# Order of a visit's output sums against the next weight part, in the last expert stage of a two-layer attention and expert kernel

## The reference, cut to what matters

```python
logits = jnp.einsum('btd,de->bte', x, Wg) + bg
top2_vals, top2_idx = jax.lax.top_k(logits, 2)
scores = jax.nn.softmax(top2_vals, axis=-1)
combine = jnp.einsum('btk,btke->bte', scores, one_hot(top2_idx))
h = gelu(jnp.einsum('btd,edh->bteh', x, W1) + b1)
y = jnp.einsum('bteh,ehd->bted', h, W2) + b2
out = jnp.einsum('bted,bte->btd', y, combine)
return _layer_norm(x + out, gamma, beta)
```

## Time and profile before

| | |
|---|---|
| median of 3 runs | 1300.97 us (1296.85 to 1301.41) |
| the profiled execution | 1300.37 us |
| its span, first to last instruction | 1298.6 us |
| mean granted TensorE clock over the span | 0.91 of full speed |
| PE matmul busy | 1131.4 us, 87% of the span |
| VectorE busy | 902.9 us, 70% |
| ScalarE busy | 790.0 us, 61% |
| GpSimd busy | 650.6 us, 50% |

### The profile page before, as it was taken

How to read it: one execution, slowest core, us unless ns; L and a number is a source line. 1 busy time by engine, 2 the same in 40 slices (tenths; PEclk the granted TensorE clock), 3 DMA queues, 4 the chain that set the end, 5 groups by cost and what they waited for, 6 DMA issues and landing times.

```text
span 1298.6 us, 23742 instructions
## 1 busy us (share of the span) xinstructions
PE 1131.4 (87%) x8184; PEld 1039.9 (80%) x8184; DVE 902.9 (70%) x1943; ACT 790.0 (61%) x1597; POOL 650.6 (50%) x581
## 2 busy tenths in 40 slices
PE   3789999998869999999988971999999999999950
PEld 2688787887858888888877861999999999999940
DVE  5677887676666666666637755787878787787847
ACT  3756566644235565565627640887878777787836
POOL 2435443443253666555443776255665745445326
PEclk8658999879999999999997865999999999999985
DMA  6544332221333778666647742568888776666649
GB/s 223 182 148 151 136 139 98 74 98 50 119 119 115 195 220 233 177 166 173 155 87 240 224 138 74 175 137 197 187 184 204 172 193 174 165 156 185 176 87 241
DMA packets 147497, 206.69 MB, mean 159 GB/s; under 512 B 29137, under 2 KB 121425, under 8 KB 140337
## 3 DMA queue, kind: packets, MB, share of 16 engines
q1 hardware_dynamic: 111376, 161.87, 38.1%
q0 software_dynamic: 35040, 42.75, 19.2%
q10 hardware_dynamic: 960, 0.54, 0.1%
HBM read 154.58 MB, written 50.53 MB: 158 GB/s over the span
## 4 chain that ended last, share of the span: by engine, by line
PE 70%; DVE 11%; ACT 6%; issue 5%; POOL 5%; DMA 2%; SPq 0%; ACTq 0%; DVEq 0%; POOLq 0%
PE quad L2029 14%; PE pb L2048 14%; PE quad L1200 13%; PE pb L1215 7%; PE quad L298 4%; PE pb L352 4%; PE pb L366 2%; POOL dSL L1882 2%; PE pb L264 1%; ACT Dm L839 1%; DVE Dm L527 1%; PE quad L2001 1%; PE quad L2023 1%; PE pb L1185 1%; PE quad L1480 1%
## 5 line engine op out<-in xcount | busy, mean ns | idle before, releaser
L2224 POOL DMA_INDIRECT dOUT<-y,es x71 | 118.9, 1675 | 192.4 <-DVE y L2130 179.5
L2048 PE MATMUL pb<-wh,hh 128*128 128x256 f32 x568 | 164.4, 289 | 1.1 <-DVE hl L2117 1.1
L2048 PE MATMUL pb<-wh,hl 128*128 128x256 f32 x568 | 160.7, 283 | 0.0
L2048 PE MATMUL pb<-wl,hh 128*128 128x256 f32 x568 | 160.6, 283 | 0.0
L1346 POOL DMA_INDIRECT dACC<-ye,idxJ x64 | 100.2, 1566 | 103.7 <-ACT ye L1310 54.7
L2186 ACT ACTIVATE gl<-quad,b1c 128x256 f32<-128x256 f32 (+1 forms) x312 | 124.6, 450 | 24.5 <-PE quad L2023 14.4
L2117 DVE TENSOR_TENSOR hl<-gl,hh 128x512 fp32r<-128x512 f32 (+1 forms) x156 | 99.6, 642 | 44.6 <-ACT hh L2191 42.5
L2029 PE MATMUL quad<-xh,wh 128*128 128x256 f32 x512 | 104.5, 286 | 8.2 <-ACT gl L2186 6.7
L2205 POOL DMA_INDIRECT xs<-dZ,es x71 | 95.9, 1351 | 28.0 <-issue 18.3
L2048 PEld LDWEIGHTS pb<-wh,hh 128*128 128x128 f32 x568 | 108.8, 192 | 1.3 <-DVE hl L2117 1.3
L2048 PEld LDWEIGHTS pb<-wl,hh 128*128 128x128 f32 x568 | 108.9, 192 | 0.0
(11 more groups left out here) (293 smaller groups left out, 3356.3 us busy)
## 6 DMA issues: line engine op xcount, KB each, us to landing
w2r<-in_W SPq DMA_DIRECT2D x39, 1024.0 KB, 5.8
MB<-dM SPq DMA_DIRECT2D x16, 1024.0 KB, 5.7
wraw<-in_Wg SPq DMA_DIRECT2D x16, 512.0 KB, 6.5
wraw<-in_Wu SPq DMA_DIRECT2D x16, 512.0 KB, 7.9
wraw<-in_Wd SPq DMA_DIRECT2D x16, 512.0 KB, 5.3
W<-in_W SPq DMA_DIRECT2D x8, 1024.0 KB, 10.7
w1p<-in_W SPq DMA_DIRECT2D x7, 1024.0 KB, 7.5
b2c<-in_b SPq DMA_DIRECT2D x39, 128.0 KB, 3.1
```

What stands on the lines that cost most here:

```text
L2048: ins = pe.matmul(bank.t[:, 0:256], a_[s][:, c, 128 * tt:128 * tt + 128], b_[n % 3][:, 256 * c:256 * c + 256], start=half == 0 and m == 0, ...
L2224: g.indirect_dma_start(out=dOUT[:, :], out_offset=bass.IndirectOffsetOnAxis(ap=es[i % 6][:, tt, 1:2].bitcast(U32), axis=0), in_=y1[i % 2][ ...
```

## The change: sums and weighing one unit later in the programs

The sums of visit i and their weighing move from the iteration of unit dn(i, 1) to that of the next unit, behind its call of `w_low` or `w_high`, which makes the part of up(i+2, 0) (none, if visit i+2 is a part visit). At the end of the stage, where the next unit's call makes the weight of dn(38, 1), the sums of visit 37 stand behind that. The last visit's sums stand behind the loop. The instructions are the same.

```diff
+            def last_sums(i):
+                v.wait_ge(*pe_t.of("dn", i, 1))
+                v.wait_ge(*b2_ld[i % 4].of(i))
+                if i >= 2:
+                    v.wait_ge(*sy_st.of(i - 2))
+                for tt in blocks(i):
+                    v.tensor_tensor(y1[i % 2][:, tt, :], banks[4 + 2 * (i % 2) + tt].t[:, 0:256], b2c[i % 4][:, :], ALU.add).then_inc(*v_t.up("y", i, tt))
+                tt = blocks(i)[-1]
+                v.wait_ge(*v_t.of("y", i, tt))
+                v.tensor_scalar(y1[i % 2][:, tt, :], y1[i % 2][:, tt, :], es[i % 6][:, tt, 0:1], None, ALU.mult).then_inc(*v_t.up("yw", i))
...
             for n, (i, kind, half) in enumerate(UNITS):
                 if n + 2 < len(UNITS):
                     w_low(n + 2)
+                if n and UNITS[n - 1][1:] == (2, 1):
+                    last_sums(UNITS[n - 1][0])
                 if kind == 1:
...
-                elif half == 1:
-                    v.wait_ge(*pe_t.of("dn", i, 1))
...
+            last_sums(VISITS - 1)
...
+            def weigh(i):
+                if width(i) == TS:
+                    a.wait_ge(*v_t.of("y", i, 0))
+                    a.activation(y1[i % 2][:, 0, :], y1[i % 2][:, 0, :], ACT.Copy, scale=es[i % 6][:, 0, 0:1]).then_inc(*a_t.up("yw", i))
+
             for n, (i, kind, half) in enumerate(UNITS):
                 if n + 2 < len(UNITS):
                     w_high(n + 2)
+                if n and UNITS[n - 1][1:] == (2, 1):
+                    weigh(UNITS[n - 1][0])
                 if kind == 1:
...
-                elif half == 1 and width(i) == TS:
-                    a.wait_ge(*v_t.of("y", i, 0))
-                    a.activation(y1[i % 2][:, 0, :], y1[i % 2][:, 0, :], ACT.Copy, scale=es[i % 6][:, 0, 0:1]).then_inc(*a_t.up("yw", i))
```

## The result

The changed kernel takes 1320.28 us (median of 5 runs, 1317.29 to 1322.03) against 1300.97 before (with two more runs, 1295.36 to 1301.83): a ratio of 1.0148, with a 95% interval of 1.0126 to 1.017 (the brackets behind the ratios below are such intervals too). Forecast were 1318.5 us and a range of 1307 to 1326.

What follows compares the result with a forecast made beforehand. PE was taken to bound the stage, with no idle time in full visits and 6.7 us of waits. Steady visits 11.9, part visits 4.3 and the end 1.9 sum to 18.1 on 1300.37: 1318.5 us, range 1307 to 1326.

Steps and rivals of the forecast that it cites:

- The delay of the GELU in a steady visit: First GELU of up(i+1, 1) on ScalarE, behind high part, low part, sums and weighing: 0.99 us later than before.
- T: Start of the first matmul of up(i+1, 1), the unit that follows dn(i, 1); times in a visit count from it.
- Steady visits, +11.9: 18 places with visits i, i+1 and i+2 full: PE waits 0.66 us each ahead of dn(i+1, 1), +11.9 us.
- Part visits, +4.3: Six places where i+1 is a part visit: net +0.53 us at the first three, +0.90 at the others, +4.3 us.
- The end, +1.9: Visit 37's sums move behind a cast and low part of dn(38, 1), its scatters go later: +1.9 us.
- The waits that were to be seen: PE waits at the down projection, put down to VectorE: some 24, 18 of about 0.66 us, 6 of about 1.85.
- The rule and the row: Skill's rule lets ScalarE's register load run ahead of a waiting instruction; the trace row disagrees, and the row decides.
- rival 1: ScalarE's register load is hidden, so the high part comes 0.58 us earlier than forecast: 1304.7 us, chance 0.10.
- Rival 2: ScalarE's register loads are slow, like the 0.647 us one, +0.37 us at 24 visits: 1327.4 us, chance 0.07.
- Rival 3: Not slower: GELU delay below 0.33 us, PE's 6.7 us of waits go: 1295.6 us, chance 0.06.
- The waits of SyncE, put at 0: SP's waits for y and for landed scatters guard loads two visits or more ahead, so they cost 0.
- VectorE's copy of the load is hidden in either order: VectorE's own register load costs nothing before or after the change; given as support for ScalarE's load being hidden.

Runs made afterwards that it cites:

- e3_two_loads: The changed kernel with ScalarE's register load done twice in a row behind the wait: 1345.09 us, ratio 1.0239 to the kernel before.
- e2_load_first: The changed kernel with ScalarE's register load ahead of the wait for dn(i, 1) instead of behind it: 1313.63 us, ratio 1.0032 to the kernel before.
- e6_parts_only: The kernel before with the change's order only at the six places where visit i+1 is a part visit: 1312.55 us, one run.
- e5_end_as_before: The changed kernel with visit 37's sums ahead of the last weight part again: 1326.3 us, one run, with 1310.27 for before on that chip.
- e7_scalar_and_loads: ScalarE's order of the change, VectorE's of before, both engines' register loads moved ahead of the part of dn(i+1, 0): 1303.31 us against 1310.27 before.
- e1_scalar_only: The changed kernel with VectorE's old order back, ScalarE keeping the new one: 1307.37 us against 1311.36 before on the same chip, ratio 0.9967.
- e4_weigh_last: The changed kernel with ScalarE's weighing behind both quarters of up(i+1, 1) instead of ahead of them: 1305.4 us, ratio 0.9945 to the kernel before.

## Why the prediction was right, point by point

- **What bounds the kernel.** Right: PE had no idle time in steady visits, and every delay of dn(i+1, 1) beyond its slack went into the time.
- **The delay of the GELU in a steady visit**, 0.99 us: measured 0.96. The register load, the one price that the trace of before showed only in its rows and not by its effect, was put at 0.58 between 0.43 and 0.64; the high part came at T + 0.85 for 0.87, and by the dose of `e3_two_loads` it is 0.54. Between the changed kernel and `e2_load_first` it is 0.56 (the high part at T + 0.85 and T + 0.29).
- **Steady visits, +11.9**: measured +13.1, by errors in opposite directions. The plain 11 lose 0.57 to 0.59 and not 0.66: 0.03 less at the GELU, 0.03 less down to the low part, and 1.28 instead of 1.32 us from that to the matmul. And I gave all 18 the slack of 0.33 us. In the seven steady visits whose i+3 is a part visit, the transposes ahead of dn(i+1, 1) are two instead of four, so that dn(i+1, 1) was due at T + 8.78 and not T + 9.00 before; with a slack of 0.11 four of these lose 0.79. The other three also met a slow register load (0.654 to 0.699 us) and lost 1.17 to 1.24. So the slack was the term that was off, and the slow loads one that the sum had left out.
- **Part visits, +4.3**: measured +4.1, and at five of the six places near the forecast. At part visit 33, up(i+2, 0) starts 3.36 us behind T instead of 4.33, so the old wait is gone, and dn(i+1, 1) 8.43 instead of 7.63: +0.80, forecast +0.90. The first two have +0.47 and +0.44 for +0.53. The third has +0.71: its load took 0.564 us before, not the 0.647 that I gave to all three, and 0.458 in the changed kernel, where it counts again. In `e6_parts_only`, without a slow load there, it has +0.54.
- **The end, +1.9**: measured +1.6; shown to be the order of visit 37's sums by `e5_end_as_before`.
- **The waits that were to be seen**: 24, in the place and with the releaser forecast, but as rows of 0.31 us (plain), 0.52 (next to a part visit; 0.91 to 0.97 with a slow load) and 1.53 (part visits), where I had written 0.66 and 1.85. What a visit loses is read from T to T (0.57, 0.79); the row of a wait is some 0.25 us short of it, as `e7_scalar_and_loads` showed too.
- **The rule and the row.** The Trainium skill (Perfetto Trace Analysis, Per-engine timelines) has the sequencer fetch the next instruction while one waits in the queue. The row of the kernel before doesn't agree: the weighing began at T + 1.51 and the load at T + 1.52, though the wait that the load itself carries was over at T + 0.18 (the semaphore's update in the trace). But I read too much into the rule when I made it rival 1's ground. In the changed kernel no instruction waits ahead of the load; the load carries the wait for dn(i, 1) itself, and starts at T + 0.20, 0.02 us behind the update at T + 0.18. So `e2_load_first` shows what the load's place costs and doesn't test the rule.
- **Rival 1, the load hidden**: doesn't hold in the changed kernel. Where it was made true, in `e2_load_first`, the stage was 5.4 us over before, for 4.3 forecast; without the 1.2 ahead of the first T it is 4.2.
- **Rival 2, slow loads everywhere**: slow loads exist, but in the stage only three (before) and four (after) are over 0.45 us.
- **Rival 3, not slower**: its condition, a GELU less than 0.33 us late, doesn't hold. `e1_scalar_only` and `e4_weigh_last` make it true, each in its own way, and both are faster than before.
- **The waits of SyncE, put at 0:** right for the changed kernel. With the scatters later still they cost 0.9 us at one unit of `e4_weigh_last`.
- **"VectorE's copy of the load is hidden in either order"**, said for rival 1: right for the two orders compared, and wrong as soon as ScalarE's high part comes early and the sums stay where they were, as `e1_scalar_only` shows.
- The sum was right to 0.4 us for the stage (18.1 against 18.5). That closeness is in part luck: the errors of the steady visits (+1.2), of the part visits (-0.2) and of the end (-0.3) and the -0.3 ahead of the first T offset one another. The remaining 1.4 us of the time lie in stages whose code is the same.

## What to carry to other kernels

Where two instructions on an engine change places, ask which of them now carries a third engine's wait to whatever is queued behind it: the part that was wanted earlier did come 1.3 us earlier here, and everything behind it came 1 us later, because the weighing took its wait for VectorE along into ScalarE's queue. The move that pays is to break the round trip and not to reorder both of its ends: put the instruction that waits for another engine's answer last (`e4_weigh_last`), or let the other engine answer first (`e1_scalar_only`). The instruction that is put last must not be one that a later load waits for with little to spare, as at visit 23 of `e4_weigh_last`. And a register load behind a wait is part of the path (0.54 us here); ahead of the wait it cost nothing.

## What the runs showed of the hardware that was not expected

- A register load with its arithmetic, behind a semaphore wait, costs 0.54 to 0.56 us on ScalarE (`e3_two_loads`; the changed kernel against `e2_load_first`), though its rows sum to 0.45 us. Ahead of the wait it was free: in `e2_load_first` it ran at T - 1.81, ahead even of two casts that stand before it in the program and started at T - 1.72 and T - 1.24. So ScalarE's sequencer went past instructions that waited only for the busy engine, but in the kernel before not past the weighing, which waited for a semaphore.
- Some loads are slow. The usual one takes 0.278 us; in the stage before, three took 0.647, 0.666 and 0.564 (at 911.6, 967.6 and 1023.7), after, four took 0.699, 0.696, 0.654 and 0.458 (at 892.5, 950.7, 1009.0 and 1032.8), and with two loads three took 0.819 to 0.850. Most come 56 us (before) or 58 us (after) apart, about one group of five visits (55.7 and 57.8), and not at the same visit in each kernel; `e4_weigh_last` and `e6_parts_only` have none on ScalarE. In the changed kernel VectorE's load, which starts at the same moment, was slow at the same four (0.722, 0.734, 0.682 and 0.489). Why they are slow wasn't tested.
